# Blocks 20 to 70 of an expert layer: the second product of a block as one-pass products of rounded halves, and a new order of the steps in a round

## The reference

```python
x = x + attention0(layernorm(x))                 # linear: theta, phi, g
h = layernorm(x)
h1 = h + attention(rmsnorm(h, ln1_w))            # causal, 16 heads, 4 of keys and values
h2 = rmsnorm(h1, ln2_w).reshape(-1, 256)
rprobs = softmax(h2 @ gate_w.T)
topw, topi = top_k(rprobs, 2)                    # 2 of 8 experts for each row, weights made to sum to 1
for e in range(8):
    g = silu(h2 @ w13[e, :512].T) * (h2 @ w13[e, 512:].T)
    out = out + (g @ w2[e].T) * wfull[:, e:e+1]
x = x + h1 + out
```

## Time and profile before

| | |
|---|---|
| three runs | 1091.48, 1093.17, 1096.17 us; median 1093.17 |
| the profiled execution | 1096.53 us, of which the span of its instructions is 1094.7 |
| TensorE busy | 1042.8 us (95%), granted clock 0.991 on average |
| VectorE, ScalarE, GpSimd busy | 754.0, 572.2, 424.2 us |

### The profile page before, as it was taken

How to read it: one execution, slowest core, us unless ns; L and a number is a source line. 1 busy time by engine, 2 the same in 40 slices (tenths; PEclk the granted TensorE clock), 3 DMA queues, 4 the chain that set the end, 5 groups by cost and what they waited for, 6 DMA issues and landing times.

```text
span 1094.7 us, 18844 instructions
## 1 busy us (share of the span) xinstructions
PE 1042.8 (95%) x6124; PEld 627.3 (57%) x6124; DVE 754.0 (69%) x1753; ACT 572.2 (52%) x1180; POOL 424.2 (39%) x480
## 2 busy tenths in 40 slices
PE   7999999999999999999999999998989999999997
PEld 6765335564435333353333444465767888888886
DVE  4699999778788897798877798135686444444443
ACT  3564576547676987648766656671431222222221
POOL 1020232615632234421534323556655753333333
PEclk9999999999999999999999999998999999999999
DMA  6333113222325557623342521232333443222221
GB/s 190 123 99 118 49 49 113 86 87 85 85 90 165 180 172 207 191 76 108 103 121 71 136 55 44 60 89 59 83 85 65 100 87 58 47 47 49 49 44 11
DMA packets 85983, 102.24 MB, mean 93 GB/s; under 512 B 17120, under 2 KB 73568, under 8 KB 85888
## 3 DMA queue, kind: packets, MB, share of 16 engines
q1 hardware_dynamic: 71584, 81.39, 25.7%
q0 software_dynamic: 14304, 19.63, 9.4%
HBM read 56.15 MB, written 41.01 MB: 89 GB/s over the span
## 4 chain that ended last, share of the span: by engine, by line
PE 69%; DVE 18%; ACT 5%; issue 5%; POOL 1%; DMA 1%; SPq 0%; DVEq 0%; POOLq 0%; ACTq 0%
PE psum L2104 10%; PE psum L2048 10%; PE psum L2034 7%; DVE psum L1820 6%; PE psum L2090 5%; PE psum L2086 4%; PE psum L2088 4%; PE psum L2087 4%; PE psum L2014 3%; PE psum L2096 3%; PE psum L2000 3%; ACT probs_mem L1355 2%; DVE mx L1822 2%; PE psum L2055 2%; PE psum L2021 2%
## 5 line engine op out<-in xcount | busy, mean ns | idle before, releaser
L1355 ACT ACTIVATE probs_mem<-psum 128x512 f32<-128x512 f32 (+1 forms) x464 | 232.6, 588 | 92.8 <-PE psum L2034 92.4
L1820 DVE CUSTOM_DVE_ANT_1 psum<-psum,masking 128x640 f32<-128x640 f32 (+3 forms) x256 | 256.5, 1047 | 30.4 <-PE psum L2017 28.9
L1254 POOL DMA_INDIRECT out<-yout,labels x71 | 114.3, 1609 | 191.1 <-DVE yout L1912 98.3
L2034 PE MATMUL psum<-stack_mem 98*128 98x512 bf16 (+3 forms) x768 | 170.8, 327 | 7.6 <-DVE mx L1820 2.8
L1374 ACT ACTIVATE gated<-psum 128x512 f32<-128x512 f32 x71 | 42.4, 598 | 248.7 <-PE psum L2088 204.9
L1203 POOL TENSOR_SCALAR_AFFINE_SELECT probs_mem<-probs_mem 128x512 f32<-128x512 f32 x104 | 66.4, 639 | 237.0 <-ACT probs_mem L1355 236.7
L2104 PE MATMUL psum<-w_mem,gated 128*128 x568 | 134.7, 380 | 0.2
L2034 PEld LDWEIGHTS psum<-stack_mem 98*128 98x128 bf16 x768 | 64.7, 97 | 104.5 <-ACT probs_mem L1355 22.1
L2104 PEld LDWEIGHTS psum<-w_mem,gated 128*128 128x128 f32 x568 | 107.7, 190 | 23.3 <-issue 7.3
L1902 DVE SCALAR_TENSOR_TENSOR gated<-gated,psum 128x512 f32<-128x512 f32 x71 | 48.7, 686 | 103.9 <-ACT gated L1374 103.9
L2048 PE MATMUL psum<-probs_mem,v 128*17 128x512 f32 (+3 forms) x1152 | 116.0, 490 | 0.7 <-ACT heads_out L1362 0.2
(11 more groups left out here) (217 smaller groups left out, 1781.1 us busy)
## 6 DMA issues: line engine op xcount, KB each, us to landing
block<-routed SPq DMA_DIRECT2D x71, 129.0 KB, 2.1
w_mem<-in_w13T SPq DMA_DIRECT2D x16, 512.0 KB, 5.2
qk_parts<-w_mem SPq DMA_DIRECT2D x16, 384.0 KB, 2.6
stack_mem<-qk_parts SPq DMA_DIRECT2D x32, 192.0 KB, 3.3
w_mem<-in_x SPq DMA_DIRECT2D x8, 512.0 KB, 5.1
out<-w_mem SPq DMA_DIRECT2D x8, 512.0 KB, 4.1
x_late<-out SPq DMA_DIRECT2D x8, 512.0 KB, 5.0
stack_mem<-qk_parts SPq DMA_DIRECT2D x32, 128.0 KB, 2.7
```

The costliest lines, as they stand in the source:

```text
L1254: e.indirect_dma_start(out_rows, bass.IndirectOffsetOnAxis(ap=labels[w % NLABEL].bitcast(I32)[:, 0:1], axis=0), youts[w % NYOUT], None, bo ...
L1355: e.activation(probs[probs_of(m)][:, hh:hh + n, q0:CH], grid(turn[step][0][:, 0:n * (CH - q0)], n), ACT.Exp, scale=float(HD) ** -0.5).then ...
L1820: e.tensor_tensor_reduce(keys, keys, masked(w), 1.0, -3e38, ALU.add, ALU.max, to).then_inc(sem["max"], 1)
L2034: m = e.matmul(bk[:, i * (CH - q0):(i + 1) * (CH - q0)], s[0:STACK + NMAX, kt // TPR, GRP, kt % TPR * P:(kt % TPR + 1) * P], s[0:STACK + N ...
```

## The change

From block 20 on (`DOWN_FROM`), `down` is made of one-pass products as the first product is: per slice of the contraction `g_hi w2_hi + g_hi w2_lo + g_lo w2_hi`, twelve matmuls of 256 columns. The rounded halves of the weights are made anew in each round, for that block's expert alone: `w2_hi` by ACT (128x1024, two buffers), `w2_lo` by DVE for the first two slices (128x512) and by POOL for the last two (`w2_part`, 128x512), into one buffer. ACT writes `g_hi` and DVE `g_lo` in place of ACT's one copy of the transposed rows. Each of the three engines reads the expert's offset into a register of its own for it.

`experts()` puts `gatedT(w - 1)` ahead of `up(w, 0)`, and `blockT(w + 1)` behind `up(w, 1)`. In the plan, durations of `up`, `w13_lo`, `label` and `w13_hi` are other numbers, and some predecessors are added. A step may be named as done when its first engine is through (`"first"`).

```diff
+DOWN_FROM = 20
+W2_PARTS = (slice(0, 2), slice(2, KF))
...
-    "fetch": (("SP", 0.6),), "label": (("POOL", 0.2),), "gatedT": (("PE", 0.44), ("ACT", 0.49)), "w13_hi": (("ACT", 0.97),),
-    "down": (("PE", 1.73), ("DVE", 0.4), ("POOL", 1.6))}
+    "fetch": (("SP", 0.6),), "label": (("POOL", 0.5),), "w13_hi": (("ACT", 1.06),), "w2_hi": (("ACT", 1.06),), "w2_lo": (("DVE", 0.87),), "w2_part": (("POOL", 1.35),),
+    }
...
-        took = sum(0.66 if is_split(w, half, k) else 0.87 for k in range(KD))
+        took = sum(0.69 if is_split(w, half, k) else 0.87 for k in range(KD))
...
+    if stage == "gatedT":
+        return (("PE", 0.44), ("ACT", 0.49), ("DVE", 0.6)) if at[0] >= DOWN_FROM else (("PE", 0.44), ("ACT", 0.49))
+    if stage == "down":
+        return ("PE", 1.38 if at[0] >= DOWN_FROM else 1.73), ("DVE", 0.4), ("POOL", 1.6)
     if stage == "w13_lo":
-        return (("POOL", 3.5),) if at[1] else (("DVE", 2.8),)
+        return (("POOL", 3.8),) if at[1] else (("DVE", 4.4),)
...
+        if stage in ("w2_lo", "w2_part"):
+            return [("w2_hi", b)] + [("first", "down", b - 1)] * (b > DOWN_FROM)
...
-            steps += [("up", w, 0)] * (w < n) + [("gatedT", w - 1)] * (w > 0) + [("blockT", w + 1)] * (w + 1 < n)
-            steps += [("up", w, 1)] * (w < n) + [("down", w - 1)] * (w > 0)
+            steps += [("gatedT", w - 1)] * (w > 0) + [("up", w, 0)] * (w < n)
+            steps += [("up", w, 1)] * (w < n) + [("blockT", w + 1)] * (w + 1 < n) + [("down", w - 1)] * (w > 0)
...
+                elif stage == "w2_part":
...
+                    q.wait_ge("w2_hi", w - DOWN_FROM + 1)
+                    if w > DOWN_FROM:
+                        q.wait_ge("down_mm", w)
+                    at_w = e.value_load(bexp[gi][0:1, c:c + 1], min_val=0, max_val=(NE - 1) * 2 * FFN)
+                    e.tensor_tensor(w2_lo[:, part], w2_mem[:, bass.ds(at_w + part.start, part.stop - part.start)], w2_hi[w % 2][:, part], ALU.subtract).then_inc(sem["w2_part"], 1)
...
+                    if w >= DOWN_FROM:
+                        q.wait_ge("down_mm", w)
+                        e.activation(g_hi, turn[step][0], ACT.Copy).then_inc(sem["g_hi"], 1)
...
+                elif stage == "w2_hi":
...
+                    if w > DOWN_FROM + 1:
+                        q.wait_ge("down_mm", w - 1)
...
+                    at_w = e.value_load(bexp[gi][0:1, c:c + 1], min_val=0, max_val=(NE - 1) * 2 * FFN)
+                    e.activation(w2_hi[w % 2], w2_mem[:, bass.ds(at_w, KF * D)], ACT.Copy).then_inc(sem["w2_hi"], 1)
...
+                elif stage == "gatedT":
+                    w, = at
+                    q.wait_ge("g_hi", w - DOWN_FROM + 1)
+                    e.tensor_tensor(g_lo, turn[step][0], g_hi, ALU.subtract).then_inc(sem["g_lo"], 1)
...
+                    if w >= DOWN_FROM:
+                        n = w - DOWN_FROM + 1
+                        q.wait_ge("g_lo", n)
+                        q.wait_ge("w2_lo", n)
+                        q.wait_ge("w2_part", n)
+                        for k in range(KF):
+                            of_k, to_k = slice(k * P, (k + 1) * P), slice(k * D, (k + 1) * D)
+                            e.matmul(bk[:, 0:D], g_hi[:, of_k], w2_hi[w % 2][:, to_k], start=(k == 0), stop=False)
+                            e.matmul(bk[:, 0:D], g_hi[:, of_k], w2_lo[:, to_k], start=False, stop=False)
+                            m = e.matmul(bk[:, 0:D], g_lo[:, of_k], w2_hi[w % 2][:, to_k], start=False, stop=(k == KF - 1))
```

More of the change, by code:

```diff
@@ L417, in needs @@
             i = at[0] * NE + at[1]
[L418 removed]
+            ready = [("split_store", NBATCH - 1, QR - 1, 2), ("x1_store", NBATCH - 1), ("v", NBATCH - 1, 1)]
+            return ready + ([("w13", (i - 4) // NE, (i - 4) % NE)] if i > 3 else [])
         if stage == "w2":
[L420 removed]
+            ready = [("split_store", NBATCH - 1, QR - 1, 2), ("x1_store", NBATCH - 1), ("v", NBATCH - 1, 1)]
             return ready + ([("w2", at[0] - 4)] if at[0] > 3 else [])
@@ L444, in needs @@
         if stage == "gatedT":
-            return [("up", b, 1), pvs[ROOMY - 1]] + [("down", b - 2)] * (b > 1)
+            return [("up", b, 1), pvs[ROOMY - 1]] + [("first", "down", b - 2)] * (b > 1)
+        if stage == "w2_hi":
+            unused = [("first", "down", b - 2)] if b > DOWN_FROM + 1 else scatter_steps(LAST - 1) + [("wo", NBATCH - 1, TPB - 1)] if b > DOWN_FROM else [("base_store", NBATCH - 1, TPB - 1)]
+            return [("w2", NE - 1), ("route", WORK[b][0], sum(route_steps(WORK[b][0])) - 1)] + unused
+        if stage in ("w2_lo", "w2_part"):
+            return [("w2_hi", b)] + [("first", "down", b - 1)] * (b > DOWN_FROM)
         if stage == "down":
-            return [("gatedT", b), ("label", b), ("w2", NE - 1), ("base_store", GROUPS[WORK[b][0]][-1], TPB - 1)]
+            halves = [("w2_lo", b), ("w2_part", b)] * (b >= DOWN_FROM)
+            return [("gatedT", b), ("label", b), ("w2", NE - 1), ("base_store", GROUPS[WORK[b][0]][-1], TPB - 1)] + halves
         return []
@@ L541, in plan @@
                (iter([(LATER + 4 * SPLIT_FROM[0, k] - 30 + ex, ("w13_hi", k, ex)) for k in range(KD) for ex in range(NE)]), False), (iter(experts()), False)]
+    streams += [(iter([(0.0, (stage, w)) for w in range(DOWN_FROM, len(WORK))]), False) for stage in ("w2_hi", "w2_lo", "w2_part")]
     streams += [(iter([(LATER + 4 * SPLIT_FROM[at] - 2, ("w13_lo", n, i)) for n, at in enumerate(QUARTERS)]), False) for i in range(2)]
@@ L669, in plan @@
         if i == 0:
+            done["first", *step] = end + DRAIN[engine]
             steps.append(step)
@@ L890, in mega_kernel @@
             "rank": lambda s: ("rank_out", 2 * nth[s]), "blockT": lambda s: ("blockT_out", nth[s]),
-            "up": lambda s: ("gated", nth[s]), "gatedT": lambda s: ("gatedT_out", nth[s]), "down": lambda s: ("y", nth[s])}
+            "up": lambda s: ("gated", nth[s]), "gatedT": lambda s: ("g_lo", nth[s] - DOWN_FROM) if s[1] >= DOWN_FROM else ("gatedT_out", nth[s]), "down": lambda s: ("y", nth[s])}
         turn, free = {}, {}
@@ L925, in mega_kernel @@
                  "pair_out", "xnT_out", "gram_out", "square_out", "hT_out", "v_out", "split_hi", "split_mid", "exp", "pv_out", "gate_wo", "gate_h",
-                 "weight_exp", "tanh", "gatedT_out", "w13_hi", "w13_lo", "w13_lo_part", "x_hi", "x_raw", "xhat", "w13", "gate_w", "square_sum",
+                 "weight_exp", "tanh", "gatedT_out", "g_hi", "g_lo", "w2_hi", "w2_lo", "w2_part", "w13_hi", "w13_lo", "w13_lo_part", "x_hi", "x_raw", "xhat", "w13", "gate_w", "square_sum",
                  "const", "wqkv", "stats", "aggr", "norm1", "xn", "x1", "stats2", "aggr2", "norm2", "h", "rope", "split_sum", "split_res", "split_lo",
```

49 lines of the change are left out of this document (41 added, 8 removed).

## The result

The changed kernel takes 1118.26 us, median of 4 runs (1117.06 to 1119.93), beside 1092.33 (1089.77 to 1096.17) for the kernel before on the same chip: ratio 1.0229, 95% interval 1.0205 to 1.0253. It is slower by 26 us; 8 had been forecast. The profiled execution took 1119.93 us, its span is 1117.0.

A forecast was written before the change was run, and what follows sets the result against it. TensorE was taken as the bound, with waits in two handover loops capping the saving. 1096.5 - 2 (quiet rounds) + 7.5 (POOL) + 1 (blocks 14 to 20) + 1.2 (fillers) + 0.4 (end) = 1104.6, less 3.4: 1101 us, range 1086 to 1113.

The forecast's parts named there:

- My own sign of being wrong: One listed sign of a wrong prediction: the stretch up to 848 us moves by more than 3 us.
- The saving: Twelve one-pass products of down at 0.116 us each: TensorE's work per round falls by 0.33 us, to 4.82.
- loop 1: Round through blockT, x_lo, the register's read and up: 4.98 us, capping the saving at 0.17 of 0.33.
- loop 2: Chain over ACT's w2_hi and g_hi, then g_lo and x_lo: 10.33 us for two rounds, round taken as 5.11.
- it fits into 5.11: In quiet rounds, POOL's read, w2_part, adding DMA and label fit into the forecast round of 5.11 us.
- I take 1.5 for each: At five places w2_part stands behind the adding DMA and delays down: 1.5 us each, +7.5 in all.
- The lock: Rival: DVE and POOL exclude each other in w2_lo and w2_part; POOL first gives 1108 us, chance 0.13.
- this stretch waits anyway, so +1: Blocks 14 to 20, one DVE copy more before x_lo, 0.25 us late seven times: +1 us, bounds 0 and 1.8.
- The fillers: 11 new filler matmuls in the attention: +1.2 us. Rival, fillers cost real time from 742 to 848: 1107, chance 0.12.
- a slow 256-column product: Rival: a 256-column product costs as much as one of 512, a round of 6.2, over 1145 us, chance 0.03.
- a TensorE that stays the bound: Rival: the read is sent ahead of x_lo or handovers are much shorter, 16 us less, 1080 us, chance 0.10.
- POOL catches up: Rival: both loops hold and POOL's late places cost nothing, rounds 4.98 to 5.11, 1088 to 1094 us, chance 0.20.

The follow-up runs named there:

- dve_read: The change with w2_lo whole on DVE, no w2_part on POOL, and TensorE's offset read ahead of the wait for x_lo: 1087.37 us, ratio 0.9922.
- dve_alone: The change with w2_lo whole on DVE and no w2_part on POOL: 1100.3 us, ratio 1.001.
- read_first: The change with TensorE's read of the expert's offset ahead of the wait for x_lo: 1109.77 us, ratio 1.0121.
- part_behind: The change with one wait more, POOL's w2_part waiting for DVE's w2_lo of the same block: 1116.91 us, ratio 1.0215.
- dve_read_late: dve_read with the old order of a round up to round 21 and the new one from 22 on: 1081.99 us, ratio 0.9857.
- numbers_only: The change without one-pass second products and with the old order of a round, keeping the plan's numbers and predecessors: 1094.54 us, ratio 0.9974.

## Why the prediction was wrong

The direction, the two places where it would be lost and the handover that caps the saving were right; the size was not, and 1118 lies outside the range. My own sign of being wrong came too: block 22 is reached 5.4 us later, and I had allowed 3 for that stretch.

- **The saving.** Right. Products of 256 columns follow one another in 0.12 us; I had taken 0.116. (The ten fillers of the earlier trace rows take 0.13 each with the last one's tail; 0.11 is the distance from start to start.) Where nothing else waits, a round falls to 4.86, near my 4.82 (dve_read, most rounds 4.86 to 4.97).
- **Loops 1 and 2.** "I take 5.11" was right for dve_alone (5.13) by luck: it came by the wrong loop. I gave loop 1 4.98 and loop 2 5.11 to 5.17. The early read removed the wait while ACT stayed as it was, so loop 1 was the longer one, and loop 2 is at most 4.93. Loop 1 was short in the term for the time from `x_lo` to the first product. My 1.27 runs to the end of that product (813.16; it starts at 812.67), which holds 0.78 until its start, from one wait; it was 0.90 in the median of dve_alone.
- **The step that failed in the quiet rounds** is "it fits into 5.11" together with the price of the read. I wrote that its long cases count, but set them at nothing in the sum, as rare ones of a median of 0.31. They are not rare. Of 32 reads recorded behind 936 us in the change, 11 take over 0.6 us and 5 more over 0.45; their mean is 0.48 us, against 0.30 in dve_alone. 33 x 0.18 = 5.9 of the 6.5 us missed there. read_first took 9.2 us out of this stretch. The trace of before had a warning in it: behind 936 us 8 of 28 reads took over 0.45 us, though nobody waited for them. What makes a read long stays open; it goes together with the end of the adding DMA's instruction on POOL half a microsecond earlier, and `w2_part` is what moved that instruction.
- **POOL at its places.** The mechanism was right and the term "I take 1.5 for each" too small. All five places were late, by 7.47 - 5.11 = 2.4 us in the mean. My chain to the end of `w2_part` was right: 5.6 us behind the end of the last `down`, measured 5.1 to 6.1, mean 5.66. Then 0.15 pass until `down` starts, which I had left out, and its end is 1.66 behind its start, where I had taken 1.39 off a round: 5.66 + 0.15 + 1.66 = 7.47. That gives 1.9 + 0.4, and I had cut the 1.9 to 1.5. What I did not have at all is the clock: the round behind block 32 ran at half clock for 3.4 us and lost 1.3. With the queue mended, 8.2 us came back between 22 and 36.
- **The lock.** It is there, and DVE is first in 40 of 46 meetings. I had said "If DVE is first, it costs nothing". Nothing here refutes that: at the late places the two don't meet, and part_behind, where they never meet, takes the same time. What it costs that `w2_part` ends 0.65 us later than alone, by the adding DMA that stands behind it, no run separates.
- **The new order up to block 22.** "this stretch waits anyway, so +1" missed 4 us at block 13. I counted `blockT`'s copies against TensorE's products only, and not against the 3 to 6 us of `w13_lo` that stand on DVE's queue there, which the same order puts ahead of them. dve_read against dve_read_late shows 3.6 us for it.
- **The fillers.** The +1.2 us in the attention is neither confirmed nor refuted: block 10 is reached at 748.3 to 751.2 us in the eight traces that have the new fillers there, and at 748.1 to 750.3 in the six that don't. From 742 us to block 22 the new ones cost nothing that is seen: numbers_only has 34 fillers there against 18 before, and takes 3 us less. That rival is out, and so are a slow 256-column product and a TensorE that stays the bound. "POOL catches up" is out too.
- **The range** treated the loops, POOL and the early stretch as separate uncertainties around a forecast that already took the mild value for each. All three went the same way, and the first two are not separate: dve_alone shows that both hang on `w2_part`.

The Trainium skill, in "SBUF — State Buffer", section "SBUF: two separate sides", says that whichever of DVE and POOL starts first keeps the shared port pair for the whole instruction. The trace agrees: where the starts lie more than 0.01 us apart, the earlier one goes first in all 34 pairs, and part_behind gives the same time with the wait written out. Of the 12 pairs that start within 0.01 us of each other by the profile, DVE goes first in 9, as at 1044.48, and POOL in 3, as here:

```profile
1001.98 1.84 DVE L1956 TENSOR_TENSOR w_lo<-w_mem,w_hi 128x512 fp32r<-128x512 f32 x1 [0.29 <-issue]
```

```profile
1001.98 1.29 POOL L1279 TENSOR_TENSOR w_lo<-w_mem,w_hi 128x512 fp32r<-128x512 f32 x1 [1.40 <-PE psum L2177]
```

## What to carry to other kernels

When work is moved to a helper engine, its price is not its own duration: add the longest wait in front of it on that engine's queue, and ask what it pushes back behind it. A read that a sequencer can do early belongs ahead of the wait for data: its long cases then cost nothing, whatever makes them. When the reads of two rounds differ, compare everything that lies at another distance from them before naming a cause; what stands at the same distance in both is not it. And an order that suits steady rounds may be wrong where large one-off operations stand in the same queue, so switch the order where those end.

## What was not expected of the hardware

- A sequencer's register read takes 0.30 us, or up to 0.74. The long ones go together with the end of an indirect DMA's instruction on POOL 0.4 to 0.7 us before (132 of 159, against 35 of 835 elsewhere), whether other engines read or not.
- TensorE stood for 2.0 us at `down(32)`, and then ran at half clock for 3.4 us: the wait cost 1.3 us more than itself.
- Splitting 1024 columns over the two engines (0.69 us on DVE, 1.8 on POOL) ends 0.6 us later than DVE alone, which takes 1.22.
